# One Mamba layer with a mixture of experts on one core: experts counted on ScalarE and GpSimd, and a new order of the work between setup and loop

## What is computed

```python
vals, idx = top_k(softmax(xf @ Wr + br), 2)
w = vals / vals.sum()
for ei in range(16):
    y = (silu(xf @ W1[ei]) * (xf @ W3[ei])) @ W2[ei]
    y = (y - mean(y)) * rsqrt(var(y) + EPS) * gamma[ei] + beta[ei]
    out += combine[:, ei:ei+1] * y
```

## Time and profile before

| | |
|---|---|
| ordinary runs shown, us | 277.14, 278.54, 1139.6 (median 278.54) |
| profiled execution, us | 276.62 |
| its span from first to last instruction, us | 274.8 |
| mean granted TensorE clock | 0.972 |
| busy share: TensorE, VectorE, ScalarE, GpSimd | 90%, 82%, 54%, 76% |
| moved over HBM | 222 GB/s over the span |

### The profile page before, as it was taken

The page is one execution under the profiler, slowest core; times in us unless marked ns, Lnnn a source line. Parts: engine busy times, 40 slices in busy tenths (PEclk is TensorE's granted clock), DMA queues, the critical chain, the costliest instruction groups (busy, mean ns, idle before and its releaser), DMA issues.

```text
span 274.8 us, 7393 instructions
## 1 busy us (share of the span) xinstructions
PE 246.5 (90%) x2158; PEld 219.3 (80%) x2158; DVE 226.1 (82%) x607; ACT 149.3 (54%) x508; POOL 209.4 (76%) x291
## 2 busy tenths in 40 slices
PE   2999997499999999999999999999999999999500
PEld 0857964498998999899989988998999899889400
DVE  4768998989888969896989789798969896986445
ACT  1765989646366363745364654547363755462033
POOL 8658997868798889878897989798788976665400
PEclk9999999799999999999999999999999999999965
DMA  5550837977869988897899897988978987870096
GB/s 161 173 151 8 271 119 218 291 205 197 259 208 265 290 256 253 258 279 227 260 284 248 253 250 216 296 261 249 304 236 255 288 258 242 220 248 20 23 280 177
DMA packets 68855, 61.55 MB, mean 224 GB/s; under 512 B 6608, under 2 KB 52304, under 8 KB 68816
## 3 DMA queue, kind: packets, MB, share of 16 engines
q1 hardware_dynamic: 66256, 55.83, 68.2%
q0 software_dynamic: 2560, 5.25, 6.8%
HBM read 56.27 MB, written 4.78 MB: 222 GB/s over the span
## 4 chain that ended last, share of the span: by engine, by line
PE 64%; POOL 5%; issue 4%; DVE 3%; DMA 3%; SPq 1%; ACT 1%; POOLq 0%; ACTq 0%; DVEq 0%
PE bank L876 18%; PE bank L921 10%; PE bank L819 5%; PE bank L871 5%; PE bank L811 4%; PE bank L835 3%; PE bank L766 2%; PE bank L853 2%; PE bank L844 2%; PE bank L771 2%; PE bank L796 2%; PE bank L803 2%; DMA decay<-res_dram 2%; PE bank L917 2%; POOL blk L583 2%
## 5 line engine op out<-in xcount | busy, mean ns | idle before, releaser
L876 PE MATMUL bank<-blkT,w_up 128*128 128x128 f32 x512 | 64.2, 279 | 0.6 <-ACT blkT L1090 0.4
L876 PEld LDWEIGHTS bank<-blkT,w_up 128*128 128x128 f32 x512 | 61.1, 195 | 1.3 <-issue 1.0
L637 POOL DMA_INDIRECT res_dram<-xrow,sidx x40 | 40.7, 1017 | 23.3 <-DVE xrow L1422 18.9
L583 POOL DMA_INDIRECT blk<-xn_dram,gidx x40 | 42.5, 1062 | 8.7 <-issue 7.6
L921 PE MATMUL bank<-w,xrow 128*128 128x128 f32 x256 | 34.7, 278 | 0.3 <-DVE xrow L1409 0.3
L921 PEld LDWEIGHTS bank<-w,xrow 128*128 128x128 f32 x256 | 31.1, 192 | 1.6 <-issue 1.6
L1096 ACT ACTIVATE xrow<-bank 128x512 f32<-128x512 f32 x40 | 24.5, 613 | 14.0 <-PE bank L876 13.7
L1326 DVE SCALAR_TENSOR_TENSOR kq<-sd,rms,bias_kq 128x512 f32<-128x512 f32 x32 | 22.7, 751 | 6.2 <-issue 4.8
L1394 DVE TENSOR_TENSOR xrow<-xrow,bank 128x512 f32<-128x512 f32 x40 | 27.2, 680 | 0.6 <-PE bank L876 0.6
L1090 ACT ACTIVATE blkT<-bank 128x128 f32<-128x128 f32 x40 | 11.6, 290 | 24.5 <-PE bank L862 24.4
L630 POOL TENSOR_TENSOR rstd<-mv,mhalf 128x1 f32<-128x1 f32 x40 | 24.5, 612 | 0.3
(11 more groups left out here) (246 smaller groups left out, 626.4 us busy)
## 6 DMA issues: line engine op xcount, KB each, us to landing
w_up<-in_L_ffn_W_dram SPq DMA_DIRECT2D x96, 256.0 KB
w<-in_L_ffn_W_dram SPq DMA_DIRECT2D x48, 256.0 KB
e_row<-e_dram SPq DMA_DIRECT2D x16, 256.0 KB, 4.0
decay<-l_dram SPq DMA_DIRECT2D x4, 512.0 KB, 5.6
gam<-in_L_ffn_gamma_dram SPq DMA_DIRECT2D x32, 64.0 KB
shift_y<-in_L_ffn_beta_dram SPq DMA_DIRECT2D x32, 64.0 KB
acc<-in_L_attn_u_dram SPq DMA_DIRECT2D x4, 256.0 KB, 3.7
xn_dram<-xrow SPq DMA_DIRECT2D x4, 256.0 KB, 5.7
```

The source lines that it names most:

```text
L583: g.indirect_dma_start(out=blk[:, b % SLOTS, :], out_offset=None, in_=xn_dram, in_offset=bass.IndirectOffsetOnAxis(ap=gidx[:, entry(b):ent ...
L637: g.indirect_dma_start(out=res_dram, in_=res[:, b % HALF, :], in_offset=None, out_offset=bass.IndirectOffsetOnAxis(ap=sidx[:, entry(b):ent ...
L876: last = m(bank[out][:, c * P:(c + 1) * P], w_up[:, u % SETS, n, c * P:(c + 1) * P], blkT[:, b % 2, :], start=True, stop=True)
```

## The change

- The count of the experts is taken from VectorE. ScalarE takes the sign of (place minus end) for the 16 ends with an accumulator, for full and mixed sets; GpSimd turns the sums of signs into twice the expert number; the transpose stands amid `sum_decays`, and the copy to `blk_e` in `one_hots(0)`. GpSimd's constants are moved by a half for it.
- GpSimd makes the turns two tiles at a time; `square_own(0)` moves behind the gathers, gather(0) ahead of the last `cut_rows`, and `weigh_q(0)` into iteration 1 behind `rms_pow(1)`.
- TensorE: `invert(1)` goes ahead of `sum_turns(2)`; two matmuls whose result isn't used precede the first block; `rise(1)` and `down(0)` go ahead of the keys; `turn_kq` is split in `turn_k` and `turn_q`.
- ScalarE: block 0's copy precedes the table load, sines and `weigh(0)` come later; `squares(0)` two tiles earlier. `gates` gives its copies of the values to `move_x`. At t = 1 `squares` precede `sines`, and `weigh` follows `silu`.
- VectorE: `mean_square(0)` precedes the wait for the inversion, the cuts of theta are in the order 0, 1, 2, 3, `diagonal(0)` comes after `product(1)`; at t = 1 `norm_kq` follows `product`. Two waits use the common step counter in place of their own.

Constants:

```diff
-    CUT = (0, 1, 3, 2)
+    CUT = (0, 1, 2, 3)
...
-        bn_kq = sd[:, 0:2, :]
+        bn_kq = sd[:, 2:4, :]
```

GpSimd:

```diff
+            pool.wait_ge(counted, 1)
+            g.tensor_scalar(behind[0:NU], full_n[0:NU], NE - 0.5, -2.0 * NE, ALU.is_gt, ALU.mult)
+            link(g.tensor_tensor(full_n[0:NU], full_n[0:NU], mix_n[0:NU], ALU.add))
+            link(g.tensor_tensor(full_n[0:NU], full_n[0:NU], behind[0:NU], ALU.add))
+            g.tensor_scalar(full_n[0:NU], full_n[0:NU], 2.0 * NE, 2.0 * (NE - 1), ALU.add, ALU.min)\
+                .then_inc(expert_ready, 1)
-            for t in range(NT):
-                last = g.tensor_tensor(turns[:, t, :].rearrange("p (h n) -> p h n", n=NA),
-                                       bc(nar[:, t, 3 * NH:3 * NH + NA], NH, 0), bc(dtp[:, t, :], NA, 1), ALU.mult)
+            for t in range(0, NT, 2):
+                last = g.tensor_tensor(turns[:, t:t + 2, :].rearrange("p t (h n) -> p t h n", n=NA),
+                                       bc(nar[:, t:t + 2, 3 * NH:3 * NH + NA], NH, 1), bc(dtp[:, t:t + 2, :], NA, 2),
+                                       ALU.mult)
...
-            square_own(0)
-            for t in range(SUMMED, NT):
+            for t in range(SUMMED, NT - 1):
                 cut_rows(t)
             pool.wait_ge(xn_out, 16 * NBATCH)
             pool.wait_ge(gidx_ready, 1)
+            gather(0)
+            cut_rows(NT - 1)
...
-            gather(0)
             gather(1)
             rms_pow(0)
-            gather(2)
-            gather(3)
+            for b in range(2, SLOTS - 2):
+                gather(b)
             rot_sine(0)
-            for b in range(4, SLOTS):
+            for b in range(SLOTS - 2, SLOTS):
                 gather(b)
+            square_own(0)
...
                 if first and t > 0:
                     rms_pow(t)
+                if t == 1:
+                    weigh_q(0)
...
-                if first:
+                if first and t > 0:
                     weigh_q(t)
```

TensorE:

```diff
             for t in range(SUMMED):
+                if t == SUMMED // 2:
+                    pe.wait_ge(expert_ready, 1)
+                    pe.wait_ge(omb_ready, 1)
+                    nc.tensor.transpose(bank[3][0:1, 0:NU], full_n[0:NU], ident[0:NU, 0:NU]).then_inc(expert_psum, 1)
                 sum_decays(t)
...
             invert(0)
-            pe.wait_ge(expert_ready, 1)
-            pe.wait_ge(omb_ready, 1)
-            nc.tensor.transpose(bank[3][0:1, 0:NU], full_n[0:NU], ident[0:NU, 0:NU]).then_inc(expert_psum, 1)
             sum_turns(1)
+            invert(1)
             sum_turns(2)
-            invert(1)
             sum_turns(3)
...
+            def begin():
+                pe.wait_ge(sidx_ready, 1)
+                for _ in range(WARM_BLOCKS):
+                    m(bank[6][:, :], ident[:, :], xnT[:, 0:512], start=True, stop=True)
+                turn_block(0)
+                pe.wait_ge(theta_ready, 2)
+                rise(0)
+                turn_block(1)
+                rise(1)
+                turn_block(2)
+                down(0)
+                turn_block(3)
+                turn_k(0)
+                state_product(0)
+                turn_q(0)
```

ScalarE:

```diff
             a(lnG, gmax, ACT.Ln).then_inc(lng_ready, 1)
+            act.wait_ge(ends_ready, 1)
+            a(cmp_f[0:NU], ends[0:NU], ACT.Sign, scale=-1.0, bias=at_full[0:NU, 0:1], accum_out=full_n[0:NU, 0:1])
+            a(cmp_m[0:NU], ends_l[0:NU], ACT.Sign, scale=-1.0, bias=from_mix[0:NU, 0:1], accum_out=mix_n[0:NU, 0:1])\
+                .then_inc(counted, 1)
...
-                if t == SUMMED + 4:
+                if t == SUMMED + 2:
                     squares(0)
...
+            def begin():
+                out_block(0)
+                nc.scalar.preload_act_table_set("silu_and_others")
+                act.wait_ge(rest_in, 16 * RESTS)
+                silu(0)
+                out_block(1)
+                sines(0)
+                silu(1)
+                out_block(2)
+                weigh(0)
+                move_x(0)
+                gates(0)
+                out_kq(0)
```

VectorE:

```diff
             link(stt(jump, ends, -2.0, ends_l, ALU.mult, ALU.add))
+            ts(from_mix, top[:, 0:1], -1.0, at_mix[:, 0:1], ALU.mult, ALU.add).then_inc(ends_ready, 1)
...
-                if k == TOPK - 1:
+                if k == 0:
                     dve.wait_ge(expert_psum, 1)
-                    v.tensor_copy(blk_e[:, :], bank[3][0:1, 0:NU]).then_inc(blk_e_ready, 1)
+                    ts(blk_e[:, :], bank[3][0:1, 0:NU], 0.5, None, ALU.mult).then_inc(blk_e_ready, 1)
...
             one_hots(0)
-            pick_experts()
             one_hots(1)
+            mean_square(0)
...
+            def begin():
+                cut_turns(0)
+                cut_turns(1)
+                cut_turns(2)
+                dve.wait_ge(rest_in, 16 * RESTS)
+                dve.wait_ge(theta_psum, 1)
+                weigh_bc(0)
+                norm_kq(0)
+                product(0)
+                rot_cosine(0)
+                rotate(0)
+                cut_turns(3)
+                product(1)
+                diagonal(0)
+                diagonal(1)
```

More of the change, by code:

```diff
@@ L243, in build @@
         zer = scratch([P, NE])
-        at_full, at_mix, full_n, mix_n, behind = (scratch([P, 1]) for _ in range(5))
+        at_full, at_mix, full_n, mix_n, behind, from_mix = (scratch([P, 1]) for _ in range(6))
         cmp_f, cmp_m = (scratch([P, NE]) for _ in range(2))
@@ L939, in iteration @@
                     down(b0 - 1)
-                if first and not begins:
+                if first:
                     project_bc(t)
@@ L943, in iteration @@
                     project_out(t - 2)
-                if b0 is not None and not begins:
+                if b0 is not None:
                     rise(b0)
@@ L948, in iteration @@
                     scores(t - 1)
-                if b0 is not None and not ends_ and not begins:
+                if b0 is not None and not ends_:
                     down(b0 - 1)
@@ L960, in iteration @@
                     turn_block(b1 + 2)
-                if first and not begins:
-                    turn_kq(t)
+                if first:
+                    turn_k(t)
+                    turn_q(t)
                 if b2 is not None:
@@ L1296, in cut_turns @@
             def cut_turns(b):
-                sums, done = bank[THETA[b]], CUT.index(b)
+                sums = bank[THETA[b]]
                 dve.wait_ge(theta_psum, b + 1)
                 cut = turns[:, b * TB:(b + 1) * TB, :].rearrange("p j c -> p (j c)") if b >= 2 else cut_[b]
-                ts(cut, sums[:, :], MAGIC, -MAGIC, ALU.add, ALU.add).then_inc(turns_cut, 1)
-                dve.wait_ge(turns_cut, done + 1)
+                link(ts(cut, sums[:, :], MAGIC, -MAGIC, ALU.add, ALU.add))
                 tt(theta[:, b * TB:(b + 1) * TB, :].rearrange("p j c -> p (j c)"), sums[:, :], cut,
@@ L1450, in iteration @@
                     add_out(t - 2)
-                if first and not begins:
-                    norm_kq(t)
+                if first:
+                    if t > 1:
+                        norm_kq(t)
                 if b0 is not None:
@@ L1462, in iteration @@
                     norm_y(b1 - 2)
-                if begins:
-                    diagonal(0)
-                elif first:
+                if first:
                     rot_cosine(t)
-                if first and not begins:
+                if first:
                     rotate(t)
```

112 lines of the change are left out of this document (45 added, 67 removed).

## The result

The changed kernel took 279.35 us in the median against 277.31 for the kernel before on the same chips: a ratio of 1.0075, with an interval from 1.0058 to 1.0091. That is 2.1 us slower, where 0.7 us faster was forecast. The measured time lies inside the range of 273.6 to 280.0; the sign is wrong. The profiled execution has a span of 277.6 us, 2.8 more than before.

What follows compares the result with a forecast made beforehand. TensorE bounds the loop; TensorE and VectorE are full from 60 to 72. Gained 4.0, given back 1.1 and 2.3: -0.6, taken as -0.7, so 275.9 profiled; plus 1.0 for ordinary runs, 276.9 us, range 273.6 to 280.0.

Steps and rivals of the forecast that it cites:

- Counting: Setup: counting experts leaves VectorE, 2.9 us off its queue; ScalarE's Signs cost zero or 0.5, GpSimd's turns take 5.6.
- Two engines that alternate: Setup one-hots: VectorE and GpSimd take turns per instruction; second long one-hot ends at 42.2, so 1.4 of 2.9 us arrive.
- rival 2: From 28 to 42 us, GpSimd's longer turns hold VectorE's slot computation and one-hots: 278.6, up to 280 us; chance 0.18.
- Inversion, gather, warm matmuls, first `rise`: Up to `project_x(1)`: block 0 turned at 48.9, `rise(0)` 2.0 us at full clock, 4.0 gained; `project_x(1)` 2.9 earlier.
- Rival 3: Clock isn't held at `rise(0)`, costing 1.3 us, or Sign needs table loads, some 2.3: 278 to 279 us; chance 0.07.
- The diagonals and iteration 1: Iteration 1: VectorE leads, TensorE waits for its results and enters the loop only 0.6 us early.
- 2.3 given back to VectorE's queue: Iteration 1: of the 2.9 us TensorE is early at `project_x(1)`, VectorE's full queue takes 2.3 back.
- The diagonals end at 60.0: Iteration 1: `square_own(0)` waits on GpSimd until 57.4, the next behind one more gather; diagonals end at 60.0, before at 61.59.
- The root of block 0 at 63.6: Iteration 1, GpSimd: root (0.73), `weigh_q(0)` (1.27), then block 0's root (0.54), done at 63.6 us.
- The keys of tile 1 are rotated at 69.0: Iteration 1, VectorE: `product(2)` starts at 63.95, `norm_kq(1)` follows with 1.4; keys rotated at 69.0 against 69.57.
- Loop and tail stay: After iteration 1: loop and tail keep their times, the loop's pairs of iterations at 25.4 us.
- Rival 1: Iteration 1: VectorE isn't the bound and the whole 2.9 us stay, giving 274.6 us; chance 0.25.

Runs made afterwards that it cites:

- spread_and_row: gathers_spread with `weigh_q(1)` behind store(2) and tile 2's root, and tile 3's row load behind block 7's weights; ratio 1.0068 to the kernel before.
- gather4_early: Changed kernel with gather(4) moved ahead of `rot_sine(0)`, into GpSimd's idle time; ratio 1.0016 to the kernel before.
- root_before_weigh: Changed kernel with the root of block 0 ahead of `weigh_q(0)` on GpSimd; ratio 1.0041 to the kernel before.
- norm_first: Changed kernel with `norm_kq(1)` ahead of `product(2)` on VectorE again; ratio 1.0020 to the kernel before.
- gather4_and_root: Changed kernel with both gather(4) ahead of `rot_sine(0)` and block 0's root ahead of `weigh_q(0)`; ratio 1.0001 to the kernel before.
- gathers_spread: norms_first with only GpSimd reordered: gathers 8 and 9 in idle times, `finish(1)` and `square_own(2)` ahead of gathers and stores; ratio 0.9992 to the kernel before.
- count_undone: Changed kernel with the experts counted on VectorE again and the sixteen small turns back; ratio 1.0154 to the kernel before.
- setup_alone: New setup with its two warm matmuls, but the start and iteration 1 of the kernel before; ratio 1.0036 to the kernel before.
- norms_first: gather4_early with norm and mean-square steps ahead of the second diagonal, and roots, `weigh_q(0)`, sine products ahead of gathers 6 to 8; ratio 1.0148 to the kernel before.
- root3_before_store: spread_and_row with the root of block 3 ahead of store(2) instead of behind it; ratio 1.0069 to the kernel before.
- no_warm: Changed kernel without the two warm matmuls ahead of block 0; ratio 1.0101 to the kernel before.

## Why the prediction was wrong, step by step

*Counting.* Right. The two Signs and their accumulators ran from 26.27 to 26.96 in ScalarE's idle time without a table load; GpSimd's four operations took 1.2 us (1.3 expected), its turns 5.06 (5.6).

*Two engines that alternate.* Nearly right. Two of VectorE's operations beside the turns took 0.72 and 0.83 us instead of 0.42, and three small ones 0.54 to 0.67: more than the nothing I charged, less than rival 2. The second long one-hot ended at 42.82 instead of 42.2. "The engines take turns, one instruction each" doesn't hold in general: in spread_and_row one shift of VectorE was held through three GpSimd instructions.

*Inversion, gather, warm matmuls, first `rise`.* Right in kind, 0.3 to 0.7 us late: first gather 45.02 (44.7), turn 49.41 (48.9), `rise(0)` in 2.02 us to 52.12 (51.5), `project_x(1)` at 57.98 (57.25). The 2.9 us gained by then were 2.16. The first weight load was out by more, 35.26 against 33.3, and the loads were not through near 46.5: the DMA share from 46.5 to 51.4 was still 0.83, against 0.92 before. The turn of block 0 had no wait for its gather all the same. Rival 3 is out: the clock was 1.00, and the table load stood at 50.02 beside `rise(0)` and took 1.28 us.

*The diagonals and iteration 1.* This step failed: "2.3 given back to VectorE's queue" measured 4.04, and another 0.7 in iteration 2, with which the sum comes out on the other side. In numbers: 0.7 less was gained up to `project_x(1)`, 1.7 more was given back in iteration 1 and 0.7 in iteration 2, which turns the -0.6 of my sum into the +2.6 measured at `project_x(3)`. The further 0.1 us that I took for the earlier weights no run shows. I treated VectorE as full and GpSimd as a few waits in between; in the changed kernel GpSimd's queue sets the pace and VectorE waits. By its terms:

- "The diagonals end at 60.0": 61.68, and this is most of the miss. ScalarE's sines ended at 53.23 instead of 52.7, and GpSimd's two sine products took 1.83 us (53.41 to 55.24) where my rows gave 1.46, so the first `square_own` ended at 58.55 instead of 57.4; the gather ahead of the second took 1.51 us instead of 1.0. The wait for the sines was in my times, but I didn't see what it meant: GpSimd idled for 2.00 us ahead of the sine products, while the gathers behind them delayed the diagonals. By gather4_early, the place of one of these gathers costs 1.56 us.
- "The root of block 0 at 63.6": done at 65.20. The terms of this chain were right: from the start of the first root to the end of this one it took 2.48 us against 2.54, and the 1.6 us are those of the diagonals. gather(7) (1.50 us at 61.05) cost nothing here, since the first root at 62.72 was released by the mean squares. root_before_weigh puts only 0.22 us on `weigh_q(0)` ahead of the root.
- "The keys of tile 1 are rotated at 69.0": 71.46, so beside the late diagonals another 0.9 us was lost from `product(2)` on: the two last rotations took 0.75 and 0.86 us instead of 0.42 beside GpSimd's work. norm_first puts 0.90 us on `norm_kq(1)` behind `product(2)`.
- "Loop and tail stay": the loop did from 97.4 us on, but iteration 2 did not. With the keys at 69.61, equal to before, gather4_and_root still had `project_x(3)` at 86.36 instead of 85.67. In both kernels the norms' root of tile 2 stands behind `weigh_q(1)`, at 77.52 there and at 76.83 before: GpSimd's queue was 0.7 us behind. That this root sets the end of iteration 2 fits the traces: `project_x(3)` comes 8.84 to 8.87 us behind it in nine kernels, from the one before (85.67 against 76.83) and the changed one (88.27 against 79.43) to gathers_spread (86.41 against 77.56), though the root itself stands anywhere from 2.26 to 4.10 us behind `project_x(2)`. It isn't shown by an edit: the kernels that tried to move the root met the shared lock or SyncE's queue instead. Why GpSimd's queue gets there late in iteration 2 stays open.

count_undone and setup_alone say the same from the other side: the counting is worth 2.2 us and arrives, and with the old order iteration 1 takes 9.49 us, so what failed is the price of the new order in iteration 1. Of its 4.04 us, 1.56, 0.90 and 0.22 are shown by edits made one at a time, and norms_first, which changes both queues, takes back 3.76; how the rest divides stays open. From the turn of block 0 to that of tile 1's keys the kernel before needed 18.2 us (69.63 - 51.40), the changed one 22.1. Rival 1 is out: TensorE had 2.54 us of idle time from 58 to 70. That this lies near the 2.3 that I forecast is luck, since the window ends ahead of the keys; the four waits shown up to them are 3.22 us, and iteration 1 grew by 4.04. Rival 2 had the right direction, and the 279.35 us measured lie within its 278.6 to 280, but its mechanism was another: GpSimd's turns holding VectorE's operations in the setup, from 28 to 42 us. Its signs didn't come (the second long one-hot ended at 42.82, the exponentials at 48.26). The loss came from VectorE waiting for results that stood late in GpSimd's queue, so that its number fits is luck too.

## What to carry to other kernels

When two engines hand work to each other through short instructions, work out the queue of both: list for each short instruction what stands ahead of it, DMA issues included, and ask of each of those whether anybody waits for it yet. A moved step that leaves an engine idle ahead of it takes along whatever stood behind it; one prefetch moved across the idle time gave back 1.6 us here. When you price an edit from a trace, count from a point that the edit can't have touched: 0.62 of the 0.84 us that root_before_weigh seemed to gain lay ahead of it. And the gain at the start must be followed until a stage that is full by itself, not only until the first point where it shows.

## What the runs showed of the hardware

- *The shared lock holds for a whole run of instructions.* A VectorE shift of 0.35 us took 1.35 beside one GpSimd product of 1.26 us, 2.71 beside three instructions in a row, and 3.15 beside three in root3_before_store, each time ending 0.15 to 0.16 us behind the last of them. The Trainium skill (SBUF — State Buffer, SBUF: two separate sides) says that the loser of the exclusive lock on the ports waits it out in full; the traces agree for one instruction, and add that a sequence without gaps counts as one.
- *An indirect DMA can cost GpSimd more beside VectorE.* In the changed kernel two gathers took 1.50 and 1.51 us, at 58.72 and 61.05, each where a diagonal of 0.69 us had begun 0.06 us ahead of it; one took 1.24 us where a rotation of 0.43 had begun 0.06 ahead (55.40). A gather that began 0.13 us ahead of VectorE's norm took 1.02 (49.03), three others up to 58 us 0.95 to 1.05, and the first of all 1.25.
- *A short idle time can cost the clock.* In count_undone and no_warm TensorE idled for 1.36 and 1.58 us ahead of the turn of block 0 and 0.41 behind it, and `rise(0)` took 3.61 us; the granted clock was 0.50 from 54 to 56 us in the first and from 50 to 52 in the second. In the changed kernel, with 0.41 us alone, it was 1.00 and `rise(0)` took 2.02 us. But 2.33 us of idle time ahead of 43.71 in count_undone and 1.38 ahead of 42.88 in the changed kernel left it at 1.00 (windows from 43.5 to 46), so the length of one gap alone doesn't tell.
